# A fused convolution and window-attention block: a smaller bottom table, moved steps and another tail

## The reference, cut to what matters

```python
x = x + conv_bn(x, dw0, groups=C)              # 3x3 depthwise
x = x + ffn(x, f0)                             # 1x1 to 128, relu, 1x1 to 64
x = x + windowed_attn(x)                       # windows of 7x7, 4 heads of 16
x = x + conv_bn(x, dw1, groups=C)
x = x + ffn(x, f1)
# in windowed_attn, per window:
q, k, v = xw @ wq.T, xw @ wk.T + pos, xw @ wv.T
q, k = focus((relu(q) + 1e-6) / sc), focus((relu(k) + 1e-6) / sc)   # focus(t) = t**3 * |t| / |t**3|
z = 1 / (q . sum(k) + 1e-6)
y = (q @ (k.T @ v)) * z + conv5x5(v)           # the depthwise 5x5 inside the window
out = y @ proj.T + proj_b
```

## Time and profile before

| | us |
|---|---|
| median of 3 runs | 197.45 (197.31 to 198.93) |
| the profiled execution, its own time | 195.69 |
| its span | 193.8 |
| mean granted clock of its PE | 0.964 of full |

### The profile page before, as it was taken

The page is one execution under the profiler, slowest core; times in us unless marked ns, Lnnn a source line. Parts: engine busy times, 40 slices in busy tenths (PEclk is TensorE's granted clock), DMA queues, the critical chain, the costliest instruction groups (busy, mean ns, idle before and its releaser), DMA issues.

```text
span 193.8 us, 4584 instructions
## 1 busy us (share of the span) xinstructions
PE 172.4 (89%) x1858; PEld 92.4 (48%) x1858; DVE 129.6 (67%) x245; ACT 89.6 (46%) x156; POOL 37.0 (19%) x79
## 2 busy tenths in 40 slices
PE   7989778899879899899899999899896989898882
PEld 6424232336516439765365365365593754532320
DVE  3744886197998793057997998998920375558551
ACT  1473454356565586233754754754742201814140
POOL 4000270053071071000700802602600000000000
PEclk9999999999999999879999999999995589999999
DMA  5999760609700000000071172162170006959922
GB/s 143 234 265 229 136 148 13 144 3 191 188 2 3 0 0 3 0 3 0 4 189 42 47 164 75 53 168 67 58 158 11 3 0 224 229 131 251 244 94 74
DMA packets 16150, 19.33 MB, mean 100 GB/s; under 512 B 3216, under 2 KB 11664, under 8 KB 16128
## 3 DMA queue, kind: packets, MB, share of 16 engines
q1 hardware_dynamic: 15552, 17.86, 38.3%
q10 hardware_dynamic: 576, 1.17, 1.9%
HBM read 14.70 MB, written 4.33 MB: 98 GB/s over the span
## 4 chain that ended last, share of the span: by engine, by line
PE 59%; DVE 15%; issue 10%; DMA 6%; ACT 6%; SPq 0%; POOL 0%; DVEq 0%; ACTq 0%; POOLq 0%
PE ps L556 7%; PE ps L546 7%; PE ps L526 7%; PE ps L583 6%; PE ps L660 5%; PE ps L685 4%; PE ps L680 4%; PE ps L628 4%; DMA x_out<-x 3%; DMA xr<-x_out 3%; PE ps L727 3%; DVE q L901 2%; PE ps L593 2%; PE ps L518 2%; ACT kv L419 2%
## 5 line engine op out<-in xcount | busy, mean ns | idle before, releaser
L354 POOL TENSOR_SCALAR vmt<-vbot,cst 128x64 f32<-128x64 f32 x48 | 16.4, 364 | 101.2 <-PE ps L620 81.3
L526 PE MATMUL ps<-xr,dwst 96*32 96x480 f32 (+1 forms) x288 | 32.1, 579 | 0.2 <-issue 0.2
L378 ACT ACTIVATE hid<-ps,fst 128x512 f32<-128x512 f32 x32 | 20.3, 686 | 22.4 <-PE ps L546 22.4
L546 PE MATMUL ps<-x,w1t 64*128 64x512 f32 x64 | 19.2, 676 | 5.1 <-ACT x L370 3.6
L556 PE MATMUL ps<-hid,w2t 128*64 128x512 f32 x64 | 19.0, 615 | 4.6 <-ACT hid L378 2.5
L419 ACT ACTIVATE kv<-ps,cst 128x288 f32<-128x288 f32 x32 | 19.4, 775 | 1.5 <-PE ps L620 1.5
L402 ACT ACTIVATE s<-t 128x1152 f32<-128x1152 f32 x8 | 9.3, 1166 | 21.9 <-DVE t L845 17.0
L344 POOL TENSOR_SCALAR vmb<-vband,cst 128x512 f32<-128x512 f32 x24 | 18.3, 778 | 0.0
L526 PEld LDWEIGHTS ps<-xr,dwst 96*32 96x32 f32 x288 | 8.3, 109 | 19.8 <-issue 18.9
L829 DVE TENSOR_TENSOR kraw<-ps,pose 128x576 f32<-128x576 f32 x8 | 6.1, 757 | 13.1 <-PE ps L593 12.8
L583 PEld LDWEIGHTS ps<-wqkv,x 64*128 64x128 f32 x128 | 11.8, 202 | 5.8 <-issue 5.8
(11 more groups left out here) (113 smaller groups left out, 263.2 us busy)
## 6 DMA issues: line engine op xcount, KB each, us to landing
xr<-x_out SPq DMA_DIRECT2D x16, 264.0 KB, 5.0
xr<-in_x SPq DMA_DIRECT2D x16, 240.0 KB, 5.4
xr<-x_out SPq DMA_DIRECT2D x8, 272.0 KB, 3.6
xr<-in_x SPq DMA_DIRECT2D x8, 256.0 KB, 4.4
out<-y SPq DMA_DIRECT2D x8, 256.0 KB, 2.4
x_out<-x SPq DMA_DIRECT2D x5, 272.0 KB, 2.1
x_out<-x ACTq DMA_DIRECT2D x3, 272.0 KB, 4.0
tband<-in_matrix SPq DMA_DIRECT2D x1, 784.0 KB, 6.6
```

Source lines behind the costliest of these rows:

```text
L354: last = eng.tensor_scalar(vmt[:, w, :], vbot[:, g, :], cc("win_bot")[:, w:w + 1], 0.0, ALU.mult, ALU.add)
L378: eng.activation(hid[:, m % 2, a, :], bank(P_H + a), ACT.Relu, bias=ff(f"f{s}b1")).then_inc(h_ready, 1)
L526: last = eng.matmul(dst[:, :, max(-dx, 0):HW - max(dx, 0)], dwst[:, s, tile % 2, dx + 1, :], taps_of(m, tile, dx), start=(dx == 0), stop=( ...
L546: eng.matmul(bank(P_H + a), w1t[p, s, :], x1[p, m % 2, :], start=True, stop=True).then_inc(h_ps, 1)
```

## The change

- `tbot` becomes 128x(16x32): a 32x32 block for each quarter, without the zeros. GpSimd's clearing of it and the wait for that go. The bottom chunk does for each of 16 `dc` four matmuls of 32x32 with 16 columns in place of one of 128x128. The tile of quarter b has rows 32b and columns 32(b ^ 2(b % 2)).
- On PE, `project_front(4)` moves from n = 5 to n = 4, behind the chunks and ahead of `ffn1(6)`. The waits for `prod_ready` and `qt_ready` move from `project_front` to `project_back`.
- On DVE, `cubes(g1)` moves from ahead of `q_sum` to behind `q_final`; `add_fm` keeps its place behind `q_sum`. The preparation of the second taps and weights moves from n = 3 to the end of n = 4.
- On ACT, `sixth(g1)` moves behind `take_kv` and `widened`.
- The tail has another order on PE, DVE and ACT, with other waits for the banks: `key_sum(7)` ahead of `attend(6)`, `key_value(7)` ahead of `conv(11)`, `take_kv(7)` ahead of `write_back(5)` and others. `project_out(5)` and `project_out(6)` change banks, `turn_fm(7)` moves to bank 7.
- Step 15: `ffn1`, relu, `ffn2`, the residual and the store work on the two column blocks j one after the other. The relu of the upper half of the hidden channels is on DVE, beside ACT's.

```diff
@@ -182,12 +182,11 @@
         tband = sb("tband", TOK, HD, TOK)
-        tbot = sb("tbot", 128, HD, 128)
+        tbot = sb("tbot", 128, HD, 32)
...
         f_in, w1_in, w2_in, c_in, t_in = sem("f_in"), sem("w1_in"), sem("w2_in"), sem("c_in"), sem("t_in")
-        t_zero = sem("t_zero")
         xr_in = [sem(f"xr_in{k}") for k in range(RING)]
@@ -201,6 +200,7 @@
         stored = sem("stored")
+        half_a, half_b = sem("half_a"), sem("half_b")
@@ -221,6 +221,12 @@
         TAPPED = 12
+        FINAL = 2 * NG - 1
+        HALF_H = ((1, 2), (3, 4))
+        HALF_F = (0, 5)
+
+        def half_of(tile, j):
+            return tile[:, PX * j:PX * j + PX]
@@ -251,10 +257,10 @@
         def project_at(g):
-            return 3 if g in (4, 5, 7) else 1
+            return 3 if g in (4, 6, 7) else 1
         def turn_bank(g):
-            return bank(2 if g < NG - 1 else 3)
+            return bank(2 if g < NG - 1 else 7)
@@ -313,10 +319,8 @@
                 load(m)
-            eng.wait_ge(t_zero, 1)
             for b in range(4):
-                q, o = slice(32 * b, 32 * b + 32), 32 * (b ^ 2 * (b % 2))
-                eng.dma_start(tbot[q, :, o:o + 32], matrix[0:32, :, 0:32]).then_inc(t_in, 16)
+                eng.dma_start(tbot[32 * b:32 * b + 32, :, :], matrix[0:32, :, 0:32]).then_inc(t_in, 16)
             eng.dma_start(tband[:, :, :], matrix).then_inc(t_in, 16)
@@ -324,15 +328,17 @@
                     store(g - 1)
-            for g in range(3, NG):
+            for g in range(3, NG - 1):
                 store(g)
-            eng.wait_ge(stored, 16 * NG)
+            for j in range(GP):
+                eng.wait_ge(res_ready, FINAL + 1 + j)
+                eng.dma_start(out_v[NG - 1][:, j], half_of(y[:, NG - 1, :], j)).then_inc(stored, 16)
+            eng.wait_ge(stored, 16 * (NG + 1))
...
             eng.memset(kv[:, 0:4, :], 0.0).then_inc(zeroed, 1)
-            eng.memset(tbot[:, :, :], 0.0).then_inc(t_zero, 1)
             eng.wait_ge(c_in, 16)
@@ -466,9 +472,9 @@
                     squares(g1)
-                sixth(g1)
                 take_kv(g2)
                 widened(n + AHEAD)
+                sixth(g1)
                 take_qt(g2)
@@ -480,16 +486,21 @@
             take_y(NG - 2)
+            take_kv(NG - 1)
             write_back(5)
             widened(LAST + AHEAD)
-            take_kv(NG - 1)
+            take_qt(NG - 1)
             write_back(6)
-            take_qt(NG - 1)
             hidden(LAST + AHEAD)
...
             write_back(7)
-            for m in range(LAST + AHEAD + 1, 2 * NG):
+            for m in range(LAST + AHEAD + 1, FINAL):
                 hidden(m)
+            eng.wait_ge(f_ps, FINAL - 1)
+            for j in range(GP):
+                eng.wait_ge(h_ps, 2 * FINAL + 2 * j + 1)
+                eng.activation(half_of(hid[:, FINAL % 2, 0, :], j), bank(HALF_H[j][0])[:, 0:PX], ACT.Relu,
+                               bias=ff("f1b1")).then_inc(half_a, 1)
@@ -506,7 +517,7 @@
                 elif m == 14:
-                    eng.wait_ge(prod_ready, NG)
+                    eng.wait_ge(ysum_ready, NG)
                 elif m == 15:
@@ -540,7 +551,8 @@
                 elif n == LAST:
-                    eng.wait_ge(x3_ready, 7)
+                    eng.wait_ge(x3_ready, 6)
+                    eng.wait_ge(ysum_ready, 7)
                 for a in range(2):
@@ -571,8 +583,6 @@
                     eng.wait_ge(kv_ready, g - 1)
-                    eng.wait_ge(prod_ready, g - 1)
-                    eng.wait_ge(qt_ready, g - 1)
                 bands(g, (0, 1))
@@ -585,6 +595,9 @@
+                if g >= 2:
+                    eng.wait_ge(prod_ready, g - 1)
+                    eng.wait_ge(qt_ready, g - 1)
                 bands(g, (2, 3))
@@ -606,7 +619,7 @@
                 if g == NG - 1:
-                    eng.wait_ge(x3_ready, 6)
+                    eng.wait_ge(x3_ready, 5)
                 if g + 1 < NG:
@@ -622,6 +635,8 @@
+                if g == NG - 1:
+                    eng.wait_ge(qt_ready, NG - 1)
                 eng.wait_ge(kf_ready, g + 1)
@@ -682,8 +697,10 @@
                     for dc in range(HD):
-                        last = eng.matmul(out_ps[:, 16 * dc:16 * dc + 16], tbot[:, dc, :],
-                                          vbot[:, gs, NH * dc:NH * dc + NH], start=True, stop=True)
+                        for b in range(4):
+                            p, o = slice(32 * b, 32 * b + 32), 32 * (b ^ 2 * (b % 2))
+                            last = eng.matmul(out_ps[o:o + 32, 16 * dc:16 * dc + 16], tbot[p, dc, :],
+                                              vbot[p, gs, NH * dc:NH * dc + NH], start=True, stop=True)
                 last.then_inc(fm_ps, 1)
@@ -692,10 +709,12 @@
                 elif g == NG - 1:
-                    eng.wait_ge(kv_ready, NG)
+                    eng.wait_ge(prod_ready, NG)
                 else:
...
                     eng.wait_ge(h_ready, 22)
+                    if g == 6:
+                        eng.wait_ge(x3_ready, 6)
                 if g >= 1:
@@ -714,12 +733,38 @@
                     eng.wait_ge(x3_ready, g)
+                if g == 5:
+                    eng.wait_ge(y_ready, 7)
+                elif g == 6:
+                    eng.wait_ge(kv_ready, NG)
                 for j in range(GP):
...
                 last.then_inc(pj_ps, 1)
+
+            def ffn1_half(j):
+
+                if j == 0:
+                    eng.wait_ge(x1_ready, FINAL + 1)
+                    eng.wait_ge(h_ready, 2 * FINAL)
+                else:
+                    eng.wait_ge(x3_ready, NG)
+                for a in range(2):
+                    p = slice(64 * a, 64 * a + 64)
+                    eng.matmul(bank(HALF_H[j][a])[:, 0:PX], w1t[p, 1, :], half_of(x1[p, FINAL % 2, :], j),
+                               start=True, stop=True).then_inc(h_ps, 1)
+
+            def ffn2_half(j):
+
+                if j == 1:
+                    eng.wait_ge(res_ready, 13)
+                for a in range(2):
+                    eng.wait_ge((half_a, half_b)[a], j + 1)
+                    last = eng.matmul(bank(HALF_F[j])[64 * a:64 * a + 64, 0:PX], w2t[:, 1, :],
+                                      half_of(hid[:, FINAL % 2, a, :], j), start=True, stop=True)
+                last.then_inc(f_ps, 1)
@@ -748,7 +793,9 @@
                 if n > 2:
-                    project_qkv(g1)
+                    if n - 1 not in FM_SLOTS:
+                        project_front(g1)
+                    project_back(g1)
                     attend(g2 - 1)
@@ -761,19 +808,21 @@
                     window_conv(k)
+                if n in FM_SLOTS and n + 1 < LAST:
+                    project_front(n)
                 ffn1(n + AHEAD)
+            key_sum(7)
             attend(6)
             turn_fm(4)
-            key_sum(7)
+            ffn2(10)
             project_out(4)
             turn_fm(5)
-            ffn2(10)
+            key_value(7)
             project_out(5)
+            conv(11)
             turn_fm(6)
-            conv(11)
-            key_value(7)
+            turn_q(7)
             project_out(6)
-            turn_q(7)
             ffn1(11)
@@ -781,11 +830,15 @@
             ffn1(12)
-            for m in range(12, 2 * NG - 1):
+            for m in range(12, FINAL):
                 conv(m + 1)
                 ffn2(m)
-                ffn1(m + 1)
-            ffn2(2 * NG - 1)
+                if m + 1 < FINAL:
+                    ffn1(m + 1)
+            ffn1_half(0)
+            ffn1_half(1)
+            ffn2_half(0)
+            ffn2_half(1)
@@ -1015,35 +1068,35 @@
                 residual(n + AHEAD - 1)
-                if n == 3:
-                    spread_taps(1).then_inc(taps_ready, 1)
-                    link(eng.tensor_scalar(mid[:, :], ff("mid"), ff("mids"), None, ALU.mult))
-                    link(eng.tensor_scalar(mid[:, 1:2], mid[:, 1:2], 1.0, None, ALU.add))
-                    scale_ffn(1)
                 q_dot(g2)
-                cubes(g1)
                 q_sum(g2)
...
                 q_final(g2)
+                cubes(g1)
                 if 0 <= c:
...
                 norm6(g1)
+                if n == 4:
+                    spread_taps(1).then_inc(taps_ready, 1)
+                    link(eng.tensor_scalar(mid[:, :], ff("mid"), ff("mids"), None, ALU.mult))
+                    link(eng.tensor_scalar(mid[:, 1:2], mid[:, 1:2], 1.0, None, ALU.add))
+                    scale_ffn(1)
             k_focus(7)
-            add_fm(4)
             q_dot(7)
             q_sum(7)
+            add_fm(4)
+            q_scale(7)
             attended(4)
...
             residual(10)
-            q_scale(7)
+            q_final(7)
             attended(5)
-            q_final(7)
+            tap_middle(4)
             add_fm(6)
             attended(6)
-            tap_middle(4)
             add_fm(7)
@@ -1057,7 +1110,16 @@
             residual(14)
-            residual(15)
```

(10 more changed lines are left out.)

## The result

The changed kernel has a median of 190.43 us (186.39 to 193.92) against 197.38 us (195.25 to 198.93) of the kernel before: ratio 0.953, 95% interval 0.941 to 0.965, faster. The forecast was 185.9 us, range 182.5 to 191.0. So the median lies 4.5 us above the forecast and 0.6 us inside the range. The ratio leaves out two disturbed executions of the changed kernel, 193.00 and the profiled one, 193.92; three others took 186.39, 187.86 and 188.12.

What follows compares the result with a forecast made beforehand. The prediction took TensorE (PE), busy 89% of the span, as the bound. Gains of 5.5 up to the clock after n = 4, 0 steady, 3.05 in n = 8 and 3.0 in the tail, 11.6 us off 197.45, gave 185.9 us, range 182.5 to 191.0.

Steps and rivals of the forecast that it cites:

- all three signs: Forecast wrong if the period moves over 0.3 us, a chunk exceeds 2.5 us, or clock shows 0.5 behind n = 8.
- Early part: n = 2 to 4: eviction order gains 0.45 us, cubes and setup moved off DVE's path 1.4, a late eviction costs 0.3.
- The front: n = 4: project_front(4) behind the chunks fills PE's wait for the bottom chunk's eviction, gaining 0.56 us.
- Bottom chunk: n = 4 and 8: small pairs 13.5 ns apart make a chunk 1.9 us, saving 1.65 and 2.0 us.
- Clock behind n = 4: After the first bottom chunk: shorter weight loading and dense work following keep full clock, gaining 1.7 us.
- Steady part: n = 5 to 8: gain 0, as ffn1 waits for attended, which ends where it did; range -1.0 to +1.5 us.
- that rival: Cubes in GpSimd's masking stretch grow by 0.4 us in each of four periods: 187.5 us; chance 0.07.
- Clock in n = 8: ffn1(10), behind the second bottom chunk, runs at full clock, gaining 1.05 us.
- Tail: From E, the end of ffn1(10), to the end: 41.4 us against 44.4 before, gaining 3.0 at full clock.
- the terms that the prediction lists for the last FFN: Step 15 in halves: ffn2, half ffn1, relu, ffn2 halves, half residual and store, written as 6.7 us against 8.1.
- The first rival: Clock falls in n = 8 anyway, key_sum and attend losing 1.4 to 3.1 us: 187.3 to 189.0; chance 0.27.
- The other rivals: Bottom chunk: pairs 25 ns apart, 193.6 us, chance 0.11; four tiles taking turns at one bank, 240 us, chance 0.05.

Runs made afterwards that it cites:

- e0: The changed kernel again, no edit, profiled once more as base of the first batch: 189.47 us.
- e13: e11 with project_front(4) back in its old place at the head of n = 5: 186.89 us, ratio 0.936 to the kernel before.
- e4: The kernel before with the small bottom table alone: 189.87 us, ratio 0.953.
- e5: The changed kernel with cubes ahead of q_sum, sixth ahead of take_kv and the setup in n = 3, as before: 190.52 us, ratio 0.985.
- e8: The changed kernel with attend(6) and turn_fm(4) ahead of key_sum(7), as in the kernel before: 188.01 us, ratio 0.961.
- e9: The changed kernel with three matmuls nobody reads, one before and two behind ffn1(10), in PE's waits: 184.38 us, ratio 0.951.
- e10: The changed kernel with 45 more tiny warm-up matmuls before conv(0), shifting the instruction stream: 187.77 us, ratio 0.972.
- e11: The changed kernel with the edits of e9, e10 (two warm-up matmuls fewer) and e2 together: 185.84 us, ratio 0.934.
- e12: e11 with the last FFN whole, in one part as in the kernel before: 185.18 us, ratio 0.937.
- e2: The changed kernel with SP holding the loads of spread(3) until both bottom chunks are done: 187.94 us.
- e3: The changed kernel with the small bottom matmuls interleaved behind each band matmul, in a bank of their own: 202.26 us.
- e1: The changed kernel with the old 128x128 bottom table and its 16 large matmuls a chunk: 195.74 us.

## Why the prediction was right, and where it was wrong

The forecast was a gain of 11.6 us. The medians show 7.0, and the executions behind the ratio 4.7%, about 9.2 us. The time fell into the range, but near its upper end, and all three signs that the prediction had named for being wrong came up in e0: the period moved by more than 0.3 us (13.9, where it was 14.3 in the mean), the chunk in n = 4 took over 2.5 us (2.78), and the clock row shows 0.50 behind n = 8. So the bottom table and its worth were understood, while the clock and the steady part were not, and errors of both signs met within a wide range. The steps, with the profile of e0 beside them:

- **Early part, 1.55 (0.45 + 1.4 - 0.3):** the bottom chunk starts at 74.61 in e0, 75.83 before: 1.2, about 0.3 short.
- **The front, 0.56:** right (e13).
- **Bottom chunk, 1.65 and 2.0:** here two errors met. The size of a pair was off: 1.26 us for 128, at most 10 ns each, not 13.5; the nearest rows were of larger tiles. And the supply of instructions was costed at nothing: it takes back 1.4 us in n = 4. So n = 4 gained 0.9 (3.72 to 2.78), and n = 8, with no tear, 2.8 (4.06 to 1.26).
- **Clock behind n = 4, 1.7:** with the small table it held in the first profile of the changed kernel, e4, e5, e8, e9, e10, e11, e12 and e13, and fell in e0 and e2 (and in e3, with its mixed shapes). With the large table it fell in both profiles, before and e1. The forecast took the loading for the cause and expected no fall behind a short chunk. The tear stands before both falls (1.41 and 0.94 us), but tears of 0.86 to 1.52 us also stand in five profiles where the clock held, so what decides in n = 4 stays open.
- **Steady part, 0:** wrong by 1.8. The step that failed is "so attended ends where it did". The cubes did take the place between `q_final` and `attended`, and `ffn1` does wait 0.33 for it, as forecast. But `q_final` itself got shorter, and so `attended` ended earlier; I had taken its stretched time as given. In three of the four passes its three pieces together took 1.68 us before and 0.93 now; in n = 6 it was 1.3 and 1.0. GpSimd still masks beside it. But `q_final` comes earlier and meets the small pieces (0.32 us each in the median) instead of the large ones (0.69). The waiting went to GpSimd's small pieces (578 ns in the mean against 364), and GpSimd has slack: 23% busy. The cubes did not grow (1.36 against 1.35), so that rival is out. This agrees with the Trainium skill's page "SBUF - State Buffer" ("SBUF: two separate sides"): when a DVE instruction with two SBUF inputs meets a GpSimd one that reads SBUF, whichever starts first holds their shared ports for its whole instruction. So a DVE piece behind a small GpSimd piece waits less than behind a large one.
- **Clock in n = 8, 1.05:** `ffn1(10)` takes 1.13 in e0: right.
- **Tail, E + 41.4:** e0 shows E + 45.8, e9 E + 41.9. The sum was right within 0.5 at full clock, down to the wait of 2.33 us (forecast 2.3), a wait of conv(14) for its loads (1.24 in e0) and the 6.8 us at the end (6.7; e12). One part of it is luck: the terms that the prediction lists for the last FFN add up to 6.25 us, not to the 6.7 that it writes. What failed is the choice that the clock holds. The first rival had the mechanism and a price of 1.4 to 3.1 us; it came true and cost 3.9, as half clock lasted from 143.9 past 152, over `key_sum`, `attend`, `turn_fm(4)` and ffn2(10). The evidence against it, full clock around a wait of 1.3 us at 179.80, was for a shorter wait, of 1.3 us and not 2.3, and so weak evidence. In e12 the clock held around one of 1.62 us, and in e13 it fell around one of 1.63, so the length of the wait alone doesn't decide either.

At E the errors nearly cancel, which is luck: before 149.4, e0 141.6, a gain of 7.8 where 8.6 was forecast. What the steady part and the chunk in n = 8 gave beyond the forecast went back in n = 4, in the chunk and the clock behind it. The rest is the tail. The other rivals are out: a pair costs 10 ns, not 25, and the four tiles don't take turns at one bank.

So of this change the table gave most (6.3 us in it, as much as the whole when alone). The other moves gave, by their stages, about 1.3 + 1.8 + 0.6 + 1.5 us, and the tail's new order, which put `key_sum(7)` first, gave 3.9 of them back to the clock.

## What to carry to other kernels

When a chain is reordered, look for the place where TensorE stands longest and ask what the clock does behind it: here 2.3 us of standing cost 3.9 us more, and three matmuls that nobody reads brought them back. A filled wait protects only its own place, as e13 shows. A block table that is mostly zeros is worth cutting to small tiles on different quarters, but keep one tile shape together. And behind a run of very short instructions look for "issue" in the timeline: a gap at a fixed count that moves with the instruction stream is supply, not data.

## What the runs showed of the hardware

- Matmuls of 16 columns on four 32x32 tiles, all into one bank and each tile into its own quarter of the partitions, follow each other at 10 ns or less (128 in 1.26 us).
- PE can run out of instructions. 106 pairs in 1.08 us were followed by 0.86 to 1.52 us of nothing in the changed kernel, e0, e2, e4, e5, e8 and e9, at the same pair each time. The page "Runtime: NRT & Kernel Launch" of the Trainium skill ("Instruction fetch mechanics") has the blocks of 256 instructions, with which the shift in e10 agrees, but calls the cost of a border mostly hidden; the trace does not agree for instructions this short.
- Changing the tile shape back and forth costs about 0.13 us a change, an estimate from one round of 0.58 us in e3.
- The granted clock can fall within a wait of 2.33 us (0.69 in its mean, e0), and half clock then lasts some 8 us.
- A DVE instruction of 128x64 with two SBUF inputs took 0.62 us beside GpSimd pieces of 0.69 us, and 0.25 us beside GpSimd pieces of 0.32 us.
- The granted clock differs between executions of one kernel: a mean of 0.946 to 0.987 in e8, 0.989 to 1.00 in e9. The time follows it.
